# Self attention of the last layer: probabilities weighed four key blocks at a time, with seven tiles, in a new order

## The reference, cut to what matters

```python
def _ada_ln(x, t, W, b):
    emb = t @ W + b
    scale, shift = jnp.split(emb, 2, axis=-1)
    mu = x.mean(-1, keepdims=True)
    var = ((x - mu) ** 2).mean(-1, keepdims=True)
    return (x - mu) * jax.lax.rsqrt(var + EPS) * (1.0 + scale) + shift

def _attn(x, ctx, Wq, Wk, Wv, Wo, bo, heads):
    q = (x @ Wq).reshape(b, n, heads, -1)
    k = (ctx @ Wk).reshape(b, j, heads, -1)
    v = (ctx @ Wv).reshape(b, j, heads, -1)
    sim = jnp.einsum('bihd,bjhd->bhij', q, k) * q.shape[-1] ** (-0.5)
    attn = jax.nn.softmax(sim, axis=-1)
    out = jnp.einsum('bhij,bjhd->bihd', attn, v).reshape(b, n, -1)
    return out @ Wo + bo

h = _ada_ln(x, t, n1_w, n1_b)
x = _attn(h, h, q1, k1, v1, o1_w, o1_b, 16) + x
```

## Time and profile before

| what | us |
|---|---|
| median of three runs | 4215.28 |
| the three runs | 4217.68, 4215.28, 4209.64 |
| the profiled execution | 4205.3 |
| its span, first to last instruction | 4203.5 |
| PE busy in the span | 3850.6 (92%) |
| DVE busy in the span | 2894.8 (69%) |
| ACT busy in the span | 2059.1 (49%) |
| POOL busy in the span | 1485.2 (35%) |
| mean granted clock of PE, as a share of 2.4 GHz | 0.962 |

### The profile page before, as it was taken

The page is one execution under the profiler, slowest core; times in us unless marked ns, Lnnn a source line. Parts: engine busy times, 40 slices in busy tenths (PEclk is TensorE's granted clock), DMA queues, the critical chain, the costliest instruction groups (busy, mean ns, idle before and its releaser), DMA issues. The chain is left out here.

```text
span 4203.5 us, 53415 instructions
## 1 busy us (share of the span) xinstructions
PE 3850.6 (92%) x19532; PEld 2316.7 (55%) x19532; DVE 2894.8 (69%) x4227; ACT 2059.1 (49%) x3724; POOL 1485.2 (35%) x850
## 2 busy tenths in 40 slices
PE   7999988899998989998999968888999999998989
PEld 6333347533334755545555446666555555546778
DVE  6888755788865667786777735555778777774465
ACT  2666655366665534443444436643444444445641
POOL 2200122220104146665666544421444444451130
PEclk8999989999998989999999989998999999999999
DMA  4233240333323333332332233232332223214320
GB/s 139 42 54 44 46 84 15 61 47 53 40 50 67 81 71 66 67 72 47 71 70 56 44 91 78 63 83 63 70 71 69 57 66 69 63 36 119 91 54 21
DMA packets 151830, 268.10 MB, mean 64 GB/s; under 512 B 33946, under 2 KB 67668, under 8 KB 150544
## 3 DMA queue, kind: packets, MB, share of 16 engines
q1 hardware_dynamic: 151568, 264.67, 29.7%
HBM read 103.96 MB, written 29.64 MB: 32 GB/s over the span
## 5 line engine op out<-in xcount | busy, mean ns | idle before, releaser
L1049 PE MATMUL PS<-t 128*128 128x512 f32 (+4 forms) x7896 | 1951.8, 378 | 108.2 <-DVE t L1705 16.5
L1509 ACT ACTIVATE t<-PS 128x512 f32<-128x512 f32 (+2 forms) x1600 | 1166.4, 750 | 1013.8 <-PE PS L1049 1005.2
L1049 PEld LDWEIGHTS PS<-t 128*128 128x128 f32 (+2 forms) x7896 | 1228.6, 184 | 629.9 <-issue 229.2
L1230 PE MATMUL PS<-t 128*32 128x512 f32 (+2 forms) x4352 | 812.6, 613 | 0.0
L1784 DVE TENSOR_REDUCE t<-PS 128x1 fp32r<-128x1024 f32 x512 | 618.2, 1218 | 238.6 <-PE PS L1121 237.8
L1790 DVE TENSOR_REDUCE t<-PS 128x1 f32<-128x512 f32 x1024 | 645.0, 681 | 58.4 <-PE PS L1125 55.0
L2090 POOL TENSOR_TENSOR t<-t 128x1024 f32<-128x1024 f32 x256 | 620.8, 2425 | 126.4 <-ACT t L1509 102.4
L1121 PE MATMUL PS<-t 128*128 128x512 f32 x1024 | 338.6, 413 | 68.3 <-DVE t L1784 35.8
L2086 POOL TENSOR_TENSOR t<-t 128x1024 f32<-128x1024 f32 x64 | 153.7, 2402 | 679.7 <-PE PS L1240 520.2
L1125 PE MATMUL PS<-t 96*128 96x512 bf16 x1024 | 357.6, 391 | 32.2 <-DVE t L1790 18.7
L1230 PEld LDWEIGHTS PS<-t 128*32 128x32 f32 (+2 forms) x4352 | 170.9, 122 | 328.8 <-issue 326.1
(11 more groups left out here) (133 smaller groups left out, 3509.3 us busy)
## 6 DMA issues: line engine op xcount, KB each, us to landing
t<-t SPq DMA_DIRECT2D x640, 128.0 KB, 2.6
t<-scr_n SPq DMA_DIRECT2D x288, 128.0 KB, 6.3
t<-t SPq DMA_DIRECT2D x128, 256.0 KB, 3.8
scr_n<-t SPq DMA_DIRECT2D x72, 256.0 KB, 2.4
t<-t SPq DMA_DIRECT2D x256, 64.0 KB, 2.1
t<-in_L_Wg SPq DMA_DIRECT2D x16, 768.0 KB, 4.5
t<-in_L_W SPq DMA_DIRECT2D x36, 256.0 KB, 3.4
t<-in_L_Wo SPq DMA_DIRECT2D x64, 128.0 KB, 2.5
```

The lines of the kernel that those rows point to most:

```text
L1049: ins = e.matmul(out, l, r, start=i == 0, stop=i == len(terms) - 1, tile_position=tp)
L1230: ins = e.matmul(banks[S.ot][wd * j:wd * j + wd, :], u.v[j][kt], P[0:S.pr, j, :], start=kt == 0, stop=kt == S.nkt - 1, tile_position=(0, w ...
L1509: e.activation(dst, src, ACT.Exp, scale=S.L.scale).then_inc(*expd.inc((S.i, i)))
```

## The change

Two constants of the stage change, and with them two waits and the place of `av`: the layer 3 self attention gets seven tiles of probabilities instead of five (`npb`), and an `av` step weighs four key blocks (`nav` = 4) after kt = 3 and kt = 7, instead of two after every second block. Layer 2, which has rotary embeddings (`L.rope`), keeps five tiles and `nav` = 2. Before, it had the same five and two.

Then the steps of stage 12 get new places by a table. Only this stage is moved.

```diff
-MOVES = {}
+MOVES = {
+    12: {
+        ('acc_v', 'self', 12): 0.059,
+        ('av', 'self'): -0.208,
+        ('max', 'self', 16, 0, 0, 0): 0.097,
+        ('max', 'self', 8): 0.026,
+        ('mturn', 'self'): -0.073,
...
+    },
+}
@@
-        S.npb = 3 if cross or L.style == 16 else 5
+        S.npb = 3 if cross or L.style == 16 else 5 if L.rope else 7
+        S.nav = 2 if L.rope else 4
@@
-                if kt % 2:
+                if kt % S.nav == S.nav - 1:
                     plan.put((i + 2.75) / k, 0, [("av", S, n, kt)])
@@
-                kts = (last - 1, last) if S.L.style == 64 and not S.cross else (last,)
+                kts = range(last + 1 - S.nav, last + 1) if S.L.style == 64 and not S.cross else (last,)
@@
-                        w.wait_ge(weighed, (S.i, pn, pkt | 1))
+                        w.wait_ge(weighed, (S.i, pn, pkt | S.nav - 1))
```

## The result

The changed kernel takes **4252.95 us**, the median of four runs (4249.98 to 4258.78); the kernel before, on the same chip, 4212.98 (4209.64 to 4217.68). The ratio is 1.0094, with a 95% interval from 1.0079 to 1.0109: slower by 0.9%, some 40 us. The forecast was 4221.8 with a range from 4204 to 4235, so it missed by 31 us, and the time lies outside the range. In the two profiled executions, the stage takes 891.9 us before (2883.39 to 3775.28, from the start of its first maximum to the start of its last `av` row) and 931.6 after (2896.35 to 3827.96). These 39.7 us are the whole effect. The two executions also differ by 13 us ahead of the stage, where both kernels have the same code: the profiled execution before was 8 us faster than its median, the one after 6 us slower.

The account below looks back on a forecast made before the run. PE was taken to bound stage 12, except where DVE sets the pace in a layer norm. The terms -9.5 + 7.9 + 8.4 - 2 + 0.7 + 1 = +6.5 us, on 4215.3, gave 4221.8 us, range 4204 to 4235.

Parts of the forecast that it names:

- the bound: Stage 12: PE has work for 814.0 of 835.0 us, so nearly all PE is spared or waits is time.
- the price of a run: Stage 12: each run of 64-column matmuls costs 0.34 us beyond its rows, whatever its length.
- Rival 4: The 0.34 goes with each two key blocks, not the run; 10.9 us is missing, 4232 us; chance 0.05.
- a choice between bounds: A sum by itself, not in the trace: surcharge between 0 and 0.34 us, taken as 0.34.
- +10.3 for the waits: First max of units 4, 20, 24, 28: waits for copies of k and q total 15.5 us against 5.2.
- +8.4 for the clock: Four waits of 3.7 to 4.1 us each drop PE's clock, losing 2.1 us in mean; from 0 to 17.
- Rival 1: Waits for the copies don't grow, as PE reaches that max late anyway; 4205 to 4206 us, faster; chance 0.24.
- rival 2: Waits for the copies grow but PE's clock holds; 4213 us; chance 0.09.
- the cover: Unit 12's first max: DVE works off older maxima while PE waits, so the longer wait costs 0 (2.6 otherwise).
- the saving of 9.5: Stage 12: fewer runs -10.9, lone transposes +3, exponential waits -3, counted for 27 of 32 units: -9.5 us.
- +1, from -4 to +8: DVE and POOL: DVE falls 1.7 us behind between double avs and recovers during the av; +1 us.
- rival 3: DVE bounds the second layer norm, a max read late behind four splits, 2 us each; 4230 us; chance 0.17.

Follow-up runs that it names:

- hidden copies: Changed kernel with the first max of units 4, 12, 20, 24 and 28 placed behind the second double av: 4228.39 us, ratio 1.0040 to the kernel before.

## Why the prediction was wrong, point by point

**Right: the bound, and the price of a run.** PE's waits are time in this stage: what the hidden copies and the single late avs take away of them comes back in the median, and what the moved bank waits do as well once the copies are hidden. The run costs 0.31 to 0.36 us (0.32 and 0.36 between starts in the changed kernel, 0.31 by the single avs, 0.29 by the joined `sum`), forecast 0.34. Rival 4 is refuted by this. The lone `sum` pays in full, which was a choice between bounds. A transpose among scores costs its 0.1.

**Right: the copies, but for unit 12.** From the first maxima of units 4, 20, 24 and 28 the forecast had +10.3 for the waits and +8.4 for the clock, less 1.4 for runs in the same units: 17.3. Units 2, 18, 22 and 26, in which they fall, are 16.5 longer. The single terms are off and offset each other: the four waits are 12.4 between starts and not 15.5, but each of these units has a bank's wait of 1.0 besides, which the forecast didn't have, and the clock cost 6.8 and not 8.4. Rival 1 (the waits don't grow) falls with the DMA waits at 16.4 us where they were 9.0, and rival 2 (the clock holds) with the rows at 0.50. The wait of unit 4 was forecast at 4.1 and is 3.5 between starts, since PE waits 1 us for a bank inside the 15 us; units 8 and 16 have none, as said, though units 6 and 14 got only 0.5 shorter and not the 3.1 that this and the runs should have given. The clock fell behind three of these four (1.7, 3.4 and 1.7 us lost at half rate) and held in one. Unit 12 was put at 0, because DVE has a backlog in the first layer norm that would cover the wait. It waited 2.66 us with the clock falling too, and unit 10 is 4.8 longer. Unit 11 is 2.0 shorter, but that is not the wait coming back: with the copies hidden unit 10 loses 4.0, and units 11 and 12 stay where they are. So the cover, which the forecast gave the whole wait, is worth nothing. Where the 2.0 come from is open; the seven tiles alone have 2.2 less in the same two units. The hidden copies give 22 to 25 us in all, where the table above has 21.4 for these five units.

**Wrong: the saving of 9.5.** Its steps were -10.9 for runs, +3 for transposes and -3 for exponentials over 32 units; 27 of 32 units of that are 9.2, a slip that doesn't matter. The first two hold as prices. The exponentials didn't get cheaper: 52 us of waits of weight loads against 31.1, where the forecast had 0.24 against 0.34 a unit moved. I had put no wait on the `av` itself, whose first weight load stands behind the exponential of its last block: 16.2 us in 41 places, and none before. An ordinary unit is 0.2 shorter and not 0.35. How much of the difference these waits make isn't shown, since a weight load overlaps PE's work. The order without the table shows the stronger case: with twice the distance between avs a `max` waits for DVE in every unit, and the runs' saving is gone.

**Missing: the bank behind a projection.** The ring of two double banks serves maxima and projections. I followed it in unit 0, where I saw 2 us gained, and nowhere else. In the new order the second next `max` comes 1.4 us after a projection whose bank is free after 2.5. It is 12.7 us of waits. Units 5, 9, 13, 17, 21 and 25 are 5.9 longer where -2 had been forecast, 8 together; moving the maxima brings back 0.6 in four of them, so that part of the 8 is another's and stays open. Unit 1 pays for its wait twice, by the clock behind it. In units 2, 10, 18 and 22 the wait cost nothing while the copies are late. This last part is shown by the lengths of these units in the two runs that move the same eleven maxima: 0.1 to 1.4 us longer where the copies are waited for, 0.2 to 0.6 shorter where they aren't. The medians agree (2 us and 8.8), but their intervals overlap.

**Mis-sized: the second layer norm.** I had +1, from -4 to +8, and as rival 3 four times 2 us of stall, with a chance of 0.17. Units 27 to 30 are 15.8 longer, more than the rival's own price. Rival 3's mechanism, a `max` read late behind a split of the layer norm, is there, but in two waits only (2.99 and 1.49 us). Two more (1.96 and 1.81) are a `max` read late behind `norm`, which no rival had, one of them left over with single avs, and 1.64 is for the copies of q in unit 28, where the kernel before had 0.75. Behind them come 13.7 us at half clock, up to 6.8 lost, which I had not priced here. My sign for this case, waits for DVE in units 26 to 30 of more than 5 us, came true. Single avs there, with the `av` at its old place, take 10.5 us off. What I had in hand to price it: a `max` every 1.5 us between two double avs, with 1.2 us of DVE for each, and no reserve for a split that takes 1.1 or 4.5 us depending on POOL. I wrote that DVE falls 1.7 us behind and recovers, and didn't add the split to the 1.7, though I named 3 us as the point from which the backlog decides.

**The sum.** Forecast +6.5, measured +39.7. By places the 33 us between are: four copies -0.8, units 6 and 14 +2.6, unit 10 +5.2, units 11 and 12 -2.0, the projections' bank +8.0, the second layer norm +15.9, ordinary units +3.6, start and end +1.0. Taking the profiled run's 10 us below the median as an offset did no harm: both stages were read from profiles. The range left out that two of the terms, "0" for unit 12 and "+1" for DVE and POOL, rest on covers, the DVE backlog and the recovery behind the `av`, and neither held.

## What to carry to other kernels

When steps are made longer and rarer to save the cost between them, look at what the engines beside PE did during the steps that were taken out: the short `av` was the time in which DVE and the copies caught up, and each wait that it hid comes out by itself. Walk every ring of buffers through the new order, with all its users, and add each rare long occupant (a layer norm, a projection) to the backlog that the forecast already has. Look also at an engine's own list: an instruction that waits there holds up a ready one behind it, as `norm` did with the maximum. And a wait that lies inside a longer transfer's time is worth nothing until the transfer is hidden: move the last wait first. What paid here was the smallest part of the change, the first `max` a few steps later, in the old order.

## What the runs showed of the hardware

- PE's clock fell behind gaps shorter than those read before, but not behind each. In the changed kernel, gaps of 1.91, 2.66 and 2.99 us (ahead of 2954.85, 3220.99 and 3750.27) were followed by 0.50 within 0.4 us. One of 2.38 us (ahead of 3680.45) was so 1.7 us later, and one of 2.37 us (ahead of 3570.60) was not. The granted clock was 1.00 in all of them. The kernel before has such a case too, 2.00 us ahead of 3263.36 and 0.50 from 3264.7 for 3.4 us.
- The length of the gap alone doesn't decide it. The wait of 1.91 us in unit 1 was followed by 0.50 in the run with hidden copies (2947.2 to 2950.4), and by 1.00 for at least 5 us in the run with single late avs, which has the same order up to unit 25. What decides isn't settled. A unit's length can differ by 1.7 us for that reason alone.
- Two short gaps near each other, 1.96 and 1.64 us with 1.6 us of work between them (ahead of 3731.25 and of 3734.56), were followed by 6.7 us at 0.50.

```profile
3733.40:3740.10 6.70, 5.54 (x14) 2.24 (x16) 3.80 (x5) 0.83 (x2) 2.40 (x1) 0.50 0.05 11
```

- A split of the layer norm on DVE takes 1.1 us, and 4.5 in unit 28, where POOL adds probabilities at the same time. Of four subtractions in the second layer norm one took 2.7 us before (mean 1.20) and two did after (mean 1.72). The order decides which of POOL's sums they meet.
